# Three groups of expert weights loaded into the homes of rounded folded weights, and half of the low parts made on GpSimd

## What is computed

```
x = x + tanh(g_xattn[0]) * mamba(ctx_1024, layernorm(x))              # scan over 256 steps
x = x + tanh(g_ffn[0])   * moe(layernorm(x))                          # 64 experts, top 8, 64 slots each
x = x + tanh(g_xattn[1]) * attention(layernorm(x), ctx_1024, mask)    # 16 heads, 8 key/value heads
x = x + tanh(g_ffn[1])   * bitnet_mlp(layernorm(x), w1, w2)            # ternary weights

def moe(hidden):                       # E = 64, K = 8, H = 256, I = 96, CAP = 64
    w, sel = top_k(softmax(x @ gate_w.T), K);  w = w / sum(w)
    slot = position of the token in its expert (dropped from CAP on)
    inp = tokens laid into expert slots
    h = silu(inp @ wg) * (inp @ wu);   out = h @ wd
    return sum over the token's choices of w * out[expert, slot]
```

## Time and profile before

| what | us |
|---|---|
| median of 3 runs | 590.9 |
| lowest and highest | 585.98, 594.54 |
| the profiled execution, span | 591.9 |
| PE busy in it | 483.0 (82%) |
| DVE busy | 473.3 (80%) |
| ACT busy | 363.3 (61%) |
| POOL busy | 281.7 (48%) |

### The profile page before, as it was taken

The page is one execution under the profiler, slowest core; times in us unless marked ns, Lnnn a source line. Parts: engine busy times, 40 slices in busy tenths (PEclk is TensorE's granted clock), DMA queues, the critical chain, the costliest instruction groups (busy, mean ns, idle before and its releaser), DMA issues.

```text
span 591.9 us, 10260 instructions
## 1 busy us (share of the span) xinstructions
PE 483.0 (82%) x3070; PEld 362.8 (61%) x3080; DVE 473.3 (80%) x1246; ACT 363.3 (61%) x830; POOL 281.7 (48%) x262
## 2 busy tenths in 40 slices
PE   5917777757668888897989999998789988999835
PEld 3302222212347756665879899997679977997614
DVE  4899999999886547976656865896898969875887
ACT  2785555436327755444756676668756697679543
POOL 3119777869310455650058538823786324323221
PEclk9956999999979999998989999999999999999876
DMA  5939300001003599998242102400135000000000
GB/s 159 228 67 338 96 0 1 1 1 35 1 9 112 196 258 297 273 274 226 75 161 70 31 0 73 65 9 2 27 64 73 2 2 2 19 2 0 1 18 19
DMA packets 45625, 48.62 MB, mean 82 GB/s; under 512 B 5660, under 2 KB 42118, under 8 KB 45574
## 3 DMA queue, kind: packets, MB, share of 16 engines
q1 hardware_dynamic: 41734, 36.46, 22.5%
q0 software_dynamic: 3840, 11.54, 8.7%
HBM read 41.43 MB, written 6.56 MB: 81 GB/s over the span
## 4 chain that ended last, share of the span: by engine, by line
PE 33%; DVE 23%; issue 22%; POOL 9%; ACT 7%; DMA 5%; DVEq 1%; POOLq 0%; ACTq 0%; another core or an unknown queue 0%
DVE hst L1798 7%; PE ps L1539 5%; PE ps L1478 4%; PE ps L1479 4%; PE ps L1480 4%; DMA G<-token_rows,idx_x 4%; PE ps L1528 3%; POOL dbu L524 2%; PE ps L1196 2%; POOL pn L619 2%; POOL G L603 2%; DVE hc L1807 2%; POOL G L581 1%; PE ps L1395 1%; PE ps L1292 1%
## 5 line engine op out<-in xcount | busy, mean ns | idle before, releaser
L619 POOL TENSOR_TENSOR pn<-pr,pinv 128x512 f32<-128x512 f32 x64 | 67.7, 1060 | 88.2 <-DVE pinv L2206 87.8
L524 POOL TENSOR_TENSOR dbu<-du,brow 128x512 f32<-128x512 f32 x64 | 81.5, 1284 | 41.5 <-DVE du L1791 23.1
L1196 PE MATMUL ps<-hc,ident 128*128 128x512 f32 x128 | 73.4, 659 | 30.7 <-DVE hc L1807 29.2
L1798 DVE TENSOR_TENSOR_SCAN hst<-ps,dbu 128x512 f32<-128x512 f32 x64 | 77.5, 1210 | 0.2 <-POOL dbu L524 0.2
L762 ACT ACTIVATE ps<-dtv,amat 128x510 f32<-128x510 f32 x64 | 44.1, 690 | 51.4 <-DVE hst L1798 50.5
L938 ACT ACTIVATE pr<-ebuf,smin 128x256 f32<-128x256 f32 x128 | 63.7, 502 | 13.5 <-POOL pn L619 6.7
L1539 PE MATMUL ps<-pT,cS 128*128 128x256 f32 x256 | 66.5, 382 | 0.0
L1196 PEld LDWEIGHTS ps<-hc,ident 128*128 128x128 f32 x128 | 20.1, 195 | 70.9 <-DVE hc L1807 68.0
L581 POOL DMA_INDIRECT G<-token_rows,idx_x x32 | 40.3, 1260 | 48.2 <-DVE wkv L1929 21.4
L603 POOL DMA_INDIRECT G<-expert_out,idx_g x48 | 51.5, 1073 | 11.6 <-issue 10.1
L2197 DVE CUSTOM_DVE_ANT_0 ebuf<-ps,mbias 128x256 f32<-128x256 f32 x128 | 48.9, 419 | 4.5 <-issue 4.4
(11 more groups left out here) (374 smaller groups left out, 1381.8 us busy)
## 6 DMA issues: line engine op xcount, KB each, us to landing
wdn<-in_L_ffn_wd SPq DMA_DIRECT2D x15, 384.0 KB, 11.0
wgu<-in_L_ffn_wg SPq DMA_DIRECT2D x14, 384.0 KB, 6.8
wgu<-in_L_ffn_wu SPq DMA_DIRECT2D x14, 384.0 KB, 10.9
expert_out<-xn SPq DMA_DIRECT2D x11, 256.0 KB, 8.5
wq<-in_L_xattn_Wq SPq DMA_DIRECT2D x2, 1024.0 KB, 8.9
wo<-in_L_xattn_Wo SPq DMA_DIRECT2D x1, 2048.0 KB, 15.4
wo<-in_L_ffn_w SPq DMA_DIRECT2D x2, 1024.0 KB, 6.7
expert_out<-pexp SPq DMA_DIRECT2D x5, 256.0 KB, 7.8
```

Of the source, the lines that this page charges most:

```text
L524: nc.gpsimd.tensor_tensor(dbu[:, j, :], du[:, j % 2, 512 * hb:512 * hb + 512], brow[:, j // 2, :], ALU.mult).then_inc(pool_dbu, 1)
L619: nc.gpsimd.tensor_tensor(pn[:, h % 2], pr[:, h % 2], pinv[:, h % 2, :].unsqueeze(2).to_broadcast([P, 2, L]), ALU.mult)\
L1196: pe.matmul(bank(2 + j % 2), ident[:], hc[:, j % 2, :], start=(isinstance(m, int) and m + k == 0), stop=(isinstance(m, int) and m + k == N ...
L1798: V.tensor_tensor_scan(hst[:, j, :], bank(j % 2), dbu[:, j, :], 0.0, ALU.mult, ALU.add)\
```

## The change

- **Homes.** `mqk0` and `nvo0` (the rounded folded weights) now lie where, before they are written, three further groups of expert weights can stand: `wgu_early0` to `2` and `wdn_early0` to `2`, for groups 5, 6 and 7 (EARLY = 3).
- **Loads.** SP issues groups 6 and 7 between the writes of the two halves of `token_rows`, once the scan's tiles there are free (`yz_ready` 2); group 5 ahead of group 4, after `idx_in_psum` 1. Groups 8 to 11 go into the four slots that groups 0 to 3 leave, groups 12 to 14 into those of 8 to 10. The steps of SP's loop in which they are issued, and the count each waits for, are written out anew.
- **The rounded copy.** `take_folded` makes the full copy only. `folded_high` on ACT makes the rounded parts from the full ones, two pieces of two heads in each of the iterations 7 to 14, after `take_out`, and counts `mn_hi`.
- **The low parts.** DVE makes those of `mqk` in four pieces of four heads, in iterations 8 to 11. GpSimd makes those of `nvo`, four pieces of four heads, after its last `take_rows`. `mn_low` counts to 8.
- **The ternary steps.** The first two of w1 move to DVE's iterations 0 and 1, the other four to 8 to 11, one each.

The core of the diff:

```diff
+        mqk_full, mqk_low = folded_pair("mqk")
+        with ExitStack() as early_scope:
+            early_gate_up, early_down = [], []
+            for g in range(EARLY):
+                early_gate_up.append(sb(f"wgu_early{g}", [P, 2, GROUP, 2 * I], F32, early_scope))
+                early_down.append(sb(f"wdn_early{g}", [P, GROUP, H], F32, early_scope))
+                if g == 0:
+                    sb("early_pad", [P, 120], F32, early_scope)
+        mqk = [sb("mqk0", [P, NH, H], F32R), mqk_low]
+        nvo = [sb("nvo0", [P, NH, H], F32R)]
...
             def gate_up_load(g):
...
-                elif RING < g < NG - 1:
-                    sp_.wait_ge(gu_done, g - RING + (g > 2 * RING))
+                elif RING + EARLY < g < NG - 1:
+                    sp_.wait_ge(gu_done, g - 7 if g < 12 else g - 3)
...
             def down_load(g):
...
-                if RING <= g < NG - 1:
-                    sp_.wait_ge(down_done, g - RING + 1)
+                if g == RING:
+                    sp_.wait_ge(down_done, 1)
+                elif RING + EARLY < g < NG - 1:
+                    sp_.wait_ge(down_done, g - 6 if g < 12 else g - 3)
...
+                if hb == 0:
+                    sp_.wait_ge(yz_ready, 2)
+                    sp_.wait_ge(d_qo, 48)
+                    sp_.wait_ge(d_kv, 32)
+                    for g in (RING + 2, RING + 3):
+                        gate_up_load(g)
+                        down_load(g)
...
+            sp_.wait_ge(d_small, 144)
+            sp_.wait_ge(idx_in_psum, 1)
+            gate_up_load(RING + 1)
+            down_load(RING + 1)
             gate_up_load(RING)
-            for g in range(NG + 2):
-                if g < RING:
-                    gate_up_load(g + RING + 1)
-                elif RING < g < NG - 1 - RING:
-                    gate_up_load(g + RING)
-                if 0 <= g - 2 < NG - 1 - RING:
-                    down_load(g - 2 + RING)
-                if g > 1:
-                    put(g - 2)
+            for s in range(NG + 2):
+                if s < 2:
+                    gate_up_load(s + 8)
+                if s == 2:
+                    down_load(RING)
+                    gate_up_load(10)
+                if s in (4, 9, 10, 11):
+                    gate_up_load(11 if s == 4 else s + 3)
+                if 2 < s < 7:
+                    down_load(s + 5)
+                if 9 < s < 13:
+                    down_load(s + 2)
+                if s > 1:
+                    put(s - 2)
...
+            for k in range(4):
+                pool.wait_ge(mn_hi, NKV + 2 * k + 2)
+                span = slice(NH // 4 * k, NH // 4 * k + NH // 4)
+                nc.gpsimd.tensor_tensor(nvo[1][:, span], nvo_full[:, span], nvo[0][:, span].bitcast(F32), ALU.subtract)\
+                    .then_inc(mn_low, 1)
...
             def take_folded(n):
...
-                A((mqk, nvo)[k][0][:, 2 * g:2 * g + 2].rearrange("p a b c -> p (a b c)" if k == 0 else "p a b -> p (a b)"),
-                  bank((n + 2) % 4), ACT.Copy)
...
+            def folded_high(n):
+                g, k = n % NKV, n // NKV
+                act.wait_ge(mn_copied, NKV * (2 - k))
+                act.wait_ge(gu_done, RING + EARLY + k)
+                act.wait_ge(down_done, RING + EARLY + k)
+                A((mqk, nvo)[k][0][:, 2 * g:2 * g + 2].rearrange("p a b c -> p (a b c)" if k == 0 else "p a b -> p (a b)"),
+                  folded[k][:, 2 * g:2 * g + 2].rearrange("p a b -> p (a b)"), ACT.Copy).then_inc(mn_hi, 1)
...
                 if g > 0:
                     take_out(g - 1)
+                if RING + EARLY <= g < RING + EARLY + NKV:
+                    for n in (2 * (g - RING - EARLY), 2 * (g - RING - EARLY) + 1):
+                        folded_high(n)
...
             def folded_low(k):
-                dve.wait_ge(mn_copied, 2 * NKV)
-                span = slice(NH // 2 * (k % 2), NH // 2 * (k % 2) + NH // 2)
+                dve.wait_ge(mn_hi, 2 * k + 2)
+                span = slice(NH // 4 * k, NH // 4 * k + NH // 4)
...
-                if 7 < g < 11:
-                    for n in (2 * g - 16, 2 * g - 15):
-                        ternary(n // 3, n % 3)
-                if 2 < g < 5:
-                    folded_low(g - 3)
-                if 10 < g < 13:
-                    folded_low(g - 9)
+                if g < 2:
+                    ternary(0, g)
+                if NT <= g < NT + 4:
+                    ternary((g - 6) // 3, (g - 6) % 3)
+                if NT <= g < NT + 4:
+                    folded_low(g - NT)
```

More of the change, by code:

```diff
@@ L54 @@
 NG = E // GROUP
+EARLY = 3
 ROW = H + E
@@ L161, in build_program, with folded_pair @@
         mamba_scope.close()
-        mqk, nvo, folded = [], [], []
-        for pair, name in ((mqk, "mqk"), (nvo, "nvo")):
-            pair.append(sb(f"{name}0", [P, NH, H], F32R))
+        def folded_pair(name):
             with ExitStack() as raw_scope:
-                folded.append(sb(f"{name}_full", [P, NH, H], F32, raw_scope))
-            pair.append(sb(f"{name}1", [P, NH, H], F32R))
+                full = sb(f"{name}_full", [P, NH, H], F32, raw_scope)
+            return full, sb(f"{name}1", [P, NH, H], F32R)
+        mqk_full, mqk_low = folded_pair("mqk")
[8 more added lines that the diff above has]
+        nvo = [sb("nvo0", [P, NH, H], F32R)]
+        nvo_full, nvo_low = folded_pair("nvo")
+        nvo.append(nvo_low)
+        folded = [mqk_full, nvo_full]
         mqk = [m[:].rearrange("p n (a b) -> p n a b", a=2) for m in mqk]
@@ L220, in gate_up_weights @@
             return (wgu[:, slot] if slot < RING else
-                    (wgu_last[:], wgu_more)[slot - RING])
+                    (wgu_last[:], wgu_more, *(w[:] for w in early_gate_up))[slot - RING])
         def gate_up_slot(g):
@@ L226, in gate_up_slot, with down_slot @@
                 return RING
[L227 to L233, removed]
-        def down_weights(slot):
-            return wdn[:, slot] if slot < RING else wdn_last[:]
+            if RING <= g <= RING + EARLY:
+                return g + 1
+            return g % RING
+        def down_weights(slot):
+            return wdn[:, slot] if slot < RING else (wdn_last[:], None, *(w[:] for w in early_down))[slot - RING]
+        def down_slot(g):
+            if g == NG - 1:
+                return RING
+            if RING < g <= RING + EARLY:
+                return g + 1
+            return g if g < RING else 0 if g == RING else (g - RING - EARLY) % RING
         G = sb("G", [P, 2, K, H])
@@ L293, in build_program, with gate_up_landed, down_landed @@
         d_w = [sem(f"d_w{k}") for k in range(RING)]
-        down_landed = ((d_ctx, 16), (d_mask, 16), (d_x, 16), (d_win, 32))
-        more_landed = (d_zero, 32)
+        down_ring = ((d_ctx, 16), (d_mask, 16), (d_x, 16), (d_win, 32))
+        early_landed = ((d_small, 144 + 48), (d_qo, 48 + 48), (d_kv, 32 + 48))
+        def gate_up_landed(g):
+            if g < RING:
+                return d_w[g], 48
+            if g == NG - 1:
+                return d_ffn, 48
+            if g == RING:
+                return d_zero, 64
+            if g <= RING + EARLY:
+                return early_landed[g - RING - 1]
+            return d_w[g % RING], 48 + 32 * (g // RING - 1)
+        def down_landed(g):
+            if g < RING:
+                return d_w[g], 48
+            if g == NG - 1:
+                return d_ffn, 48
+            if RING < g <= RING + EARLY:
+                return early_landed[g - RING - 1]
+            s, before = down_ring[down_slot(g)]
+            return s, before + 16 * (1 if g < 12 and g != 11 else 2)
         d_rows = sem("d_rows")
@@ L1409, in down @@
             def down(g):
-                slot = g % RING if g < NG - 1 else RING
-                if RING <= g < NG - 1:
-                    pe.wait_ge(down_landed[slot][0], down_landed[slot][1] + 16 * (g // RING))
+                slot = down_slot(g)
+                pe.wait_ge(*down_landed(g))
                 pe.wait_ge(hT_ready, g + 1)
@@ L1500, in queries @@
                 if b == 0 and h == 0:
-                    pe.wait_ge(mn_low, 4)
+                    pe.wait_ge(mn_low, 8)
                     pe.wait_ge(wternT_ready, 4)
@@ L2038, in folded_low @@
             def folded_low(k):
-                dve.wait_ge(mn_copied, 2 * NKV)
-                span = slice(NH // 2 * (k % 2), NH // 2 * (k % 2) + NH // 2)
[L2042 to L2045, removed]
+                dve.wait_ge(mn_hi, 2 * k + 2)
+                span = slice(NH // 4 * k, NH // 4 * k + NH // 4)
+                high, low = (d[:, span].rearrange("p a b c -> p (a b c)") for d in mqk)
+                V.tensor_tensor(low, mqk_full[:, span].rearrange("p a b -> p (a b)"), high.bitcast(F32), ALU.subtract)\
+                    .then_inc(mn_low, 1)
             def gated(g):
@@ L2297, in hidden @@
                 wait_count(dve, f_hq, 2 * f)
-                dve.wait_ge(d_kv, 32 + 64)
```

(1 more changed line is left out.)

18 lines of the change are left out of this document (8 added, 10 removed).

## The result

The changed kernel takes 587.4 us in the median of 20 runs (584.6 to 591.1), the kernel before 590.9 on the same chip (20 runs, 586.0 to 594.5): 0.9941 of it, 95% interval 0.9918 to 0.9963. That is 3.5 us faster, where 9.4 were forecast. On a second chip it was 0.9943 (0.9919 to 0.9967).

The account below looks back on a forecast made before the run. The expert stage was taken to be PE work from end to end, losing 10.2 us to waits for eo_lo and gathered rows and a lower clock. -10.2 - 1.5 + 1.3 + 1.0 = -9.4 us gave 581.5 us, range 577 to 587.5.

Parts of the forecast that it names:

- The middle of the stage, -10.2: Expert groups 4 to 15: loads moved forward return all 10.2 us of PE's lost time; bounds 4 and 10.2.
- The fold, -1.5: End of the fold: one of ACT's copies per product removed, saving 1.5 us; bounds 0.6 and 2.0.
- GpSimd against DVE, +1.3: Expert iterations 10 and 11: GpSimd's subtractions hold up DVE's eo_lo, about half of one hit, 1.3 us; bounds 0 and 10.
- Gathers, +1.0: Iterations 9 to 11: the last four gathers meet subtraction, rounding and compressed loads, costing 1.0 us; bounds 0 and 3.2.
- Charged nothing: Expert stage: ACT's remade rounded copies, DVE's moved work and token_rows landing some 3 us later were each charged 0.
- Clean relief: Expert stage: no collision and rows of groups 3 to 5 land sooner, 12 to 13.7 us gained, 577 to 579; chance 0.17.
- The late results: Expert stage: results still land late behind the weights of groups 12 to 14, only 4 us gained, 587; chance 0.15.
- GpSimd against DVE: Expert stage: each of four GpSimd subtractions blocks an eo_lo for its length, 10 us paid, 590 to 592; chance 0.08.
- The clock: Iterations 10 to 14: new stalls bring PE to half speed, up to 4.46 us more per iteration; chance 0.05.

Follow-up runs that it names:

- fold_alone: Kernel before with everything of the change but homes and loads, all low parts on DVE in iterations 8 to 15: 0.9990 of before.
- low_on_dve: Changed kernel with all low parts made on DVE, none on GpSimd: 583.9 and 583.2 us, 0.9908 and 0.9885 of before.
- pool_halves: Changed kernel with the GpSimd subtractions cut into eight pieces of two heads instead of four of four: 585.97 us, 0.9929 of before.
- late_67: Changed kernel with groups 6 and 7 loaded at the start of the expert stage, behind groups 5 and 4: 0.9997 of before.

## Why the prediction was right or wrong

The direction and the mechanism of the loads came out; the size did not: 3.5 us instead of 9.4.

**The middle of the stage, -10.2: the step that failed.** The mechanism is right: no wait for writes is left, and with the GpSimd pieces away g4 to g15 comes down to 49.42 and 48.95, close to the floor of 48.4 that was worked out. But the term took the whole loss of one execution for what returns each time, and the upper end of its own bounds (4 to 10.2). The mean of the four traces of before is 54.90, so about **-5.7** was there to gain. In that execution g8 to g15 took 37.87, in the three others 31.7 to 34.2. There was a place to ask: 591.9 us of span was set beside a median of 590.9 us of run time as "1 us above", but the two are not the same measure, and by the estimate above the execution was about 3 us above. Also not all of it came from the loads: about 2.3 of the 5.7 (g4 to g8, 20.95 in the mean of before, 18.68) are there in fold_alone too, where the two subtractions are out of iterations 3 and 4 and the loads stayed. Why before scatters by 6 us from g8 to g15 these runs don't show; ACT's waits for writes go with it (4.5 to 14.1 us).

**The fold, -1.5.** Measured -1.8 in every trace (17.07 to 15.26). Within its bounds.

**GpSimd against DVE, +1.3.** Measured +4.0 by the traces (2.8 and 1.2, above), 2 to 3 by the timed runs, within 0 to 10. The step that failed is which row meets the subtraction. The prediction looked for eo_lo, and of the eo_lo only one (279.65) begins during a subtraction. But place and the rounding step do in the three other cases, and they stand ahead of the next eo_lo on DVE's queue. They have one tensor operand in SBUF, and the only row it had of such a meeting was an addition of two. The Trainium skill (SBUF — State Buffer, "Who interferes with whom") names them too: copies and tensor_scalar operations can enter a mode that takes the ports shared with GpSimd. The trace agrees (place 0.61 to 2.70, the rounding step 1.22 to 2.73); the prediction had drawn on the page for two-input operations alone. The piece's length, 2.5 us, was right (2.37 to 2.73), and so was that it ends before the first query product.

**Gathers, +1.0.** Not seen: PE's wait for rows is 2.4 us, against 4.7, 2.9, 2.1 and 3.2 in the four traces of before, and the gathers of after land sooner than those of the earlier trace rows:

```profile
DMA to landing us min/median/max: 2.9/5.3/7.1
```

**Charged nothing.** folded_high held: 16 copies of 0.61 us, and nobody but GpSimd's subtractions waits for them. DVE's iterations 8 to 11 stay at 4.45 us until GpSimd starts. The second half of token_rows, behind the early loads, delays nothing: the first row transposes come 1.8 us earlier, the whole of the fold's gain.

**The sum by the runs.** g0 to g4 -0.6 (17.34 to 16.77 in the means), then -5.7, -1.8 and +4.0: -4.1, against -3.5 and -3.4 by the timed runs. The sum ends at the first query product; from there to the end of the span the fourteen traces take 291.5 to 294.7 us, before 292.7 and after 293.7 in the mean, so the agreement is no closer than that scatter. Attention takes 246.76 us from its first value product to its last, before 246.77.

**The rivals.** Clean relief fell with the four meetings; even without them low_on_dve stays at 583 to 584 us, above its 577 to 579. The late results (587) hit the number by another way: ACT waits for none. GpSimd against DVE, the right mechanism, was given 0.08 as an all-or-nothing case at 10 us; here it is 4. The clock fell where its rival put it, in the last iterations, in two of the three traces of after, but to 0.83 and 0.84 over 10 us, not to half for two iterations.

## What to carry to other kernels

Before a stall is priced, look at the same stretch in more than one execution, compare span with span, and ask how much of the loss returns every time. Work handed to an idle GpSimd is not free while DVE is on the way to the end: count every DVE instruction with all its operands in SBUF that can begin during it (those were held here), by what stands behind each in the queue, not only the one that is awaited. Loads that were to run early had to be out before the first gathers too.

## What the runs showed of the hardware that was not expected

- Six GpSimd subtractions in a row (13.9 us) kept a DVE rounding step of 1.22 us waiting through all of them: 14.46 us. DVE got no turn between them. Cut into halves that wait for a semaphore each, it got one in one case and not in another.
- A copy of 64x2, 0.35 us for a pair, takes 2.47 beside two GpSimd subtractions of 128x512 (pool_halves). The gate product `gated`, which reads one operand from PSUM, kept its 0.35 us beside one (263.54 in the changed kernel).
- One wait of 2.4 us of PE was followed by full clock in one execution of the changed kernel and by 0.83 and 0.84 over the next 10 us in the two others, with gate products of 2.83 and 2.07 us instead of 1.52. In late_67 it was 0.83 behind a wait of 2.40, in pool_halves 0.83 behind one of 1.57. What decides these runs don't tell.
